# Layer 2's scan: delta*u of every fourth unit by an fp32 product on PE, y stores on ACT's queue

## The reference

```
def step(state, inp):
    d, b, c, uu = inp
    dA = jnp.exp(d[..., None] * A_neg[:, None, :, :])
    state = dA * state + (d * uu)[..., None] * b[:, :, None, :]
    y = jnp.einsum('kbcn,kbn->kbc', state, c)
    return (state, y)
```

## Time and profile before

| | |
|---|---|
| median of 3 runs | 17231.57 us (17228.62 to 17241.57) |
| profiled execution | 17236.15 us |
| its span, first to last instruction | 17234.5 us |
| scan of layer 2 | 8540 to 15594 us of the span |
| granted PE clock, mean over the span | 0.833 |
| PE busy over the span | 12704.4 us (74%) |
| DVE busy | 11266.0 us (65%) |
| ACT busy | 7765.1 us (45%) |
| POOL busy | 6782.0 us (39%) |

### The profile page before, as it was taken

One profiled execution on the slowest core, in us unless ns is written; L12 is line 12 of the kernel. 1 busy time (PEld: TensorE's weight loads), 2 busy tenths in 40 slices (PEclk: granted clock), 3 DMA queues, 4 the chain that ended last, 5 costly groups with the idle time before them and its releaser, 6 DMA issues. The chain is left out here.

```text
span 17234.5 us, 361490 instructions
## 1 busy us (share of the span) xinstructions
PE 12704.4 (74%) x127392; PEld 8742.7 (51%) x127392; DVE 11266.0 (65%) x10439; ACT 7765.1 (45%) x13769; POOL 6782.0 (39%) x3199
## 2 busy tenths in 40 slices
PE   7889999888999954454466666666666666667799
PEld 5666666666666632222244444444444444444477
DVE  5666666666666655555477777777777777775532
ACT  4444444444444434544455545554555545552200
POOL 1000000000000014423577777887778877772100
PEclk9999999999999977777677777777777777776799
DMA  5222222222222237766899999999999999998711
GB/s 124 65 57 58 59 59 53 66 56 66 59 59 59 53 106 186 179 153 159 209 233 233 234 230 233 235 235 234 236 232 235 237 228 232 233 230 222 197 39 40
DMA packets 2038805, 2633.89 MB, mean 153 GB/s; under 512 B 1083612, under 2 KB 1935324, under 8 KB 2013404
## 3 DMA queue, kind: packets, MB, share of 16 engines
q1 hardware_dynamic: 1991388, 2487.10, 59.5%
q0 software_dynamic: 12288, 86.71, 2.3%
q10 hardware_dynamic: 34944, 57.81, 1.2%
HBM read 2103.61 MB, written 556.32 MB: 154 GB/s over the span
## 5 line engine op out<-in xcount | busy, mean ns | idle before, releaser
L1731 DVE TENSOR_TENSOR_SCAN L2.h<-L2.ps,L2.db 128x912 f32<-128x912 f32 x2688 | 5515.0, 2056 | 1569.2 <-POOL L2.db L1587 1522.1
L1587 POOL TENSOR_TENSOR L2.db<-L2.du,L2.bt 128x896 f32<-128x896 f32 x2688 | 5580.1, 2096 | 1551.7 <-DMA L2.du<-du 1468.0
L1608 PE MATMUL L2.ps<-L2.dm,L2.wa 32*128 32x112 f32 x21504 | 2306.9, 346 | 2471.1 <-DVE L2.h L1731 2343.4
L1669 ACT ACTIVATE L2.ps<-L2.ps 128x896 f32<-128x896 f32 x2688 | 2424.5, 902 | 3503.4 <-PE L2.ps L1608 3501.6
L1608 PEld LDWEIGHTS L2.ps<-L2.dm,L2.wa 32*128 32x128 f32 x21504 | 1899.6, 246 | 3268.2 <-DVE L2.h L1731 2940.3
L1621 PE MATMUL L2.ps<-L2.h,L2.cd 128*8 128x96 f32 x50176 | 2575.6, 362 | 5.5 <-DVE L2.h L1731 5.5
L1621 PEld LDWEIGHTS L2.ps<-L2.h,L2.cd 128*8 128x8 f32 x50176 | 1439.4, 108 | 583.6 <-DVE L2.h L1731 5.6
L314 POOL TENSOR_TENSOR L1.x_res<-L1.x_res,L1.ob 96x3136 f32 (+1 forms) x16 | 95.4, 5977 | 2582.2 <-ACT L1.qv L457 2582.2
L314 POOL TENSOR_TENSOR L0.x_res<-L0.x_res,L0.ob 96x3136 f32 (+1 forms) x16 | 95.9, 6007 | 2367.8 <-ACT L0.qv L457 2367.8
L366 PE MATMUL L1.p_proj<-L1.xt,L1.w_hi 128*96 128x448 f32 x3024 | 826.4, 383 | 194.2 <-DVE L1.xt L560 167.5
L366 PE MATMUL L0.p_proj<-L0.xt,L0.w_hi 128*96 128x448 f32 x3024 | 826.3, 383 | 194.3 <-DVE L0.xt L560 167.6
(11 more groups left out here) (255 smaller groups left out, 19811.4 us busy)
## 6 DMA issues: line engine op xcount, KB each, us to landing
L2.du<-du SPq DMA_DIRECT2D x5376, 224.0 KB, 6.6
L2.dm<-d SPq DMA_DIRECT2D x896, 336.0 KB, 6.8
y<-L2.ysum SPq DMA_DIRECT2D x896, 84.0 KB
L0.left<-table SPq DMA_DIRECT2D x48, 1176.0 KB
L0.right<-table SPq DMA_DIRECT2D x48, 1176.0 KB
L1.left<-table SPq DMA_DIRECT2D x48, 1176.0 KB
L1.right<-table SPq DMA_DIRECT2D x48, 1176.0 KB
du<-L2p.work SPq DMA_DIRECT2D x64, 784.0 KB, 7.5
```

What stands on the lines that cost most here:

```text
L1587: pool.tensor_tensor(db[:, n % RB, :, 2:ROW], du[:, n % RD, :].rearrange("p (c t) -> p c t", t=SPAN), row, ALU.mult)\
L1608: mm = pe.matmul(decays[n % RA][:, lo:lo + SPAN], wa[rows, u * QUAD + e, :], dm[rows, u * QUAD + e, :], start=True, stop=True)
L1669: act.activation(a, a, ACT.Exp).then_inc(a_ready, 1)
L1731: dve.tensor_tensor_scan(h[:, half, u * UNIT:(u + 1) * UNIT, :].rearrange("p c t -> p (c t)"), decays[n % RA], db[:, n % RB, :, :].rearran ...
```

## The change

In the scan of layer 2:
- Units with n % 4 = 3 (six of a span's 24) get no `load_du`. SP loads the eight images' rows once (`load_few`, two runs of 1,792 B for each of 8 partitions) into `few`, which has two slots. It is issued at unit n = 4i for unit 4i + 3. PE multiplies them with `fan`, an 8 x 128 matrix of zeros and ones, in fp32 (`fan_out`): two products of 448 columns, at the ends of units 4i and 4i + 1, both into bank 7. ACT copies each into the unit's slot of `du` (`copy_du`) before the decay of units 4i + 1 and 4i + 2. POOL waits for these copies (`du_copied`) instead of a transfer.
- The sums have bank 6 alone; `sum_states` waits until ACT has taken the fill before.
- On ACT `take_sum` stands before the unit's decay and carry instead of behind them.
- `ysum` has one buffer. Its stores are issued from ACT's queue, behind u = 11 of the half in which the sums were made (and before `make_cd`), and ACT waits at u = 4 of the next half for the stores to have landed.

```
+        def by_pe(n):
+            return n % 4 == 3
...
-                    load_du(k, s, half, u)
-                    if u == 2 and earlier is not None:
-                        sp.wait_ge(sum_out, fills + (2 - FILLS))
-                        steady(sp)
-                        store_y(*earlier, half)
+                    n = half * UNITS + u
+                    if n % 4 == 0:
+                        load_few(k, s, n // 4)
+                    if not by_pe(n):
+                        load_du(k, s, half, u)
...
+            def fan_out(i, g, k, s):
+                copies = count(pe, k, s, 2 * FANS, 2 * i + g)
+                if g == 0:
+                    pe.wait_ge(few_in[i % 2], count(pe, k, s, 16 * FANS // 2, 16 * (i // 2 + 1)))
+                if not (isinstance(copies, int) and copies == 0):
+                    pe.wait_ge(du_copied, copies)
+                pe.matmul(ps[:, 7, 0:QUAD * SPAN], fan[:], few[:, i % 2, g * QUAD * SPAN:(g + 1) * QUAD * SPAN],
+                          start=True, stop=True).then_inc(fanned, 1)
...
-                bank = 6 + (half * FILLS + f) % 2
-                pe.wait_ge(sum_out, fills + (f + 1))
+                pe.wait_ge(sum_out, fills + (f + 2))
...
                         sum_states(1 - half, f, before)
+                    n = half * UNITS + u
+                    if n % 4 < 2:
+                        fan_out(n // 4, n % 4, k, s)
...
+            def copy_du(i, g, units, copies):
+                n = 4 * i + 3
+                act.wait_ge(fanned, copies + (2 * i + g + 1))
+                act.wait_ge(b_ready, units + (n + 1))
+                act.copy(du[:, n % RD, g * QUAD * SPAN:(g + 1) * QUAD * SPAN], ps[:, 7, 0:QUAD * SPAN]).then_inc(du_copied, 1)
...
                 for u in range(UNITS):
-                    decay(half * UNITS + u, spreads)
-                    carry(half, u, units, begun)
                     f = u - FIRST_FILL - 1
                     if 0 <= f < FILLS and not first:
                         if f == 0:
-                            act.wait_ge(y_stored[1 - half], count(act, k, s, 64, 64 * half))
+                            act.wait_ge(y_stored[half], count(act, k, s, 64, 64))
                         take_sum(k - 1 if begun and half == 0 else k, 1 - half, f, before)
+                    n = half * UNITS + u
+                    if 1 <= n % 4 <= 2:
+                        copy_du(n // 4, n % 4 - 1, units, copies)
+                    decay(n, spreads)
+                    carry(half, u, units, begun)
+                if not first:
+                    act.wait_ge(sum_out, before + (FILLS + 2))
+                    steady(act)
+                    if half:
+                        store_y(k, s, 0)
+                    elif begun:
+                        store_y(k - 1, NSPANS - 1, 1)
+                    else:
+                        store_y(k, act.snap(s - 1), 1)
                 if half == 0:
                     make_cd(k, s, before)
```

More of the change, by code:

```diff
@@ L1420, in scan_layer @@
         db = m.sb("db", [128, RB, UNIT, ROW])
-        ysum = m.sb("ysum", [128, 2, SPAN // 4, HALF])
+        ysum = m.sb("ysum", [128, SPAN // 4, HALF])
+        few = m.sb("few", [BATCH, 2, UNIT * SPAN])
+        fan = m.sb("fan", [BATCH, 128])
         zero = m.sb("zero", [128, UNIT])
@@ L1432, in scan_layer @@
         bt_in = [m.sem(f"bt_in{s}") for s in range(2)]
+        few_in = [m.sem(f"few_in{s}") for s in range(2)]
+        fanned = m.sem("fanned")
+        du_copied = m.sem("du_copied")
         image_in = m.sem("image_in")
@@ L1454, in count @@
             return eng.snap(s * scale + (k * NSPANS * scale + add))
+        def by_pe(n):
+            return n % 4 == 3
+        FANS = 2 * UNITS // 4
+        moved = [[n for n in range(2 * UNITS) if n % RD == q and not by_pe(n)] for q in range(RD)]
         def span_of(s):
@@ L1488, in load_cc, with load_few @@
                 sp.dma_start(cc[:], bc_dram[1, k].rearrange("b n t -> (b n) t")[:, span_of(s)]).then_inc(cc_in, 16)
+            def load_few(k, s, i):
+                before = count(sp, k, s, 2 * FANS, 2 * (i - 1))
+                n = 4 * i + 3
+                c = n // UNITS * HALF + n % UNITS * QUAD
+                rows = du_dram[k, :, 0, 0:NSPANS * CH * SPAN].rearrange("b (s g n) -> b s g n", s=NSPANS, n=SET * SPAN)
+                g0, at = c // SET, c % SET * SPAN
+                rows = rows[:, s, g0:g0 + 2, at:at + QUAD * SPAN] if isinstance(s, int) else \
+                    rows[:, bass.ds(s, 1), g0:g0 + 2, at:at + QUAD * SPAN].rearrange("b a g n -> b (a g) n")
+                if not (isinstance(before, int) and before <= 0):
+                    sp.wait_ge(fanned, before)
+                steady(sp)
+                sp.dma_start(few[:, i % 2, :].rearrange("b (g n) -> b g n", g=2), rows).then_inc(few_in[i % 2], 16)
             def load_du(k, s, half, u):
@@ L1499, in load_du, with half_span @@
                     sp.dma_start(du[:, slot, g * QUAD * SPAN:(g + 1) * QUAD * SPAN], src).then_inc(du_in[slot], 16)
[L1501 to L1510, removed]
+            def half_span(k, s, half, later, table):
                 units = count(sp, k, s, 2 * UNITS, half * UNITS)
-                fills = count(sp, k, s, 2 * FILLS, half * FILLS)
                 for u in range(UNITS):
@@ L1578, in span @@
                 units = count(pool, k, s, 2 * UNITS)
-                loads = count(pool, k, s, 32 * 2 * UNITS // RD)
+                loads = {q: count(pool, k, s, 32 * len(moved[q])) for q in range(RD) if moved[q]}
+                copies = count(pool, k, s, 2 * FANS)
                 for half in range(2):
@@ L1584, in span @@
                         n = half * UNITS + u
[L1585 removed]
+                        if by_pe(n):
+                            pool.wait_ge(du_copied, copies + 2 * (n // 4 + 1))
+                        else:
+                            pool.wait_ge(du_in[n % RD], loads[n % RD] + 32 * (moved[n % RD].index(n) + 1))
                         pool.wait_ge(scanned, units + (n + 1))
@@ L1655, in _, with store_y @@
             act.wait_ge(cleared, 1)
-            act.wait_ge(image_in, 16)
+            act.wait_ge(image_in, 32)
+            def store_y(k, s, half):
+                for q in range(4):
+                    at = s * SPAN + SPAN // 4 * q
+                    if k % 2:
+                        at = at * -1 + (TOK - SPAN // 4)
+                    rows = slice(at, at + SPAN // 4) if isinstance(s, int) else bass.ds(at, SPAN // 4)
+                    place = y_dram[k, :, rows, half * HALF:(half + 1) * HALF]
+                    act.dma_start(place, ysum[32 * q:32 * q + BATCH, :, :]).then_inc(y_stored[half], 16)
             def make_cd(k, s, fills):
```

27 lines of the change are left out of this document (14 added, 13 removed).

## The result

The changed kernel takes 16,749.85 us (median of four runs, 16,740.79 to 16,755.04), beside 17,234.71 us (17,228.62 to 17,241.57) for the kernel before on the same chip. The ratio is 0.9724, with a 95% interval of 0.9712 to 0.9736: 485 us less, where 17,250 us, no change, had been forecast. The profiled execution has a span of 16,739.1 us. Times "on the mean" or "as a median" over halves are taken over 107 halves of each kind (half 0, half 1) in the profiled execution of the kernel named.

The account below looks back on a forecast made before the run. Du loads over DMA bound layer 2's scan; afterwards a PE and ACT chain of 31.1 us per half, 31.3 with late loads, times 224 plus 5 and some 35 gives 7,051 against 7,054 us: 17,250 us, range 16,600 to 17,750.

Parts of the forecast that it names:

- What bounds the kernel now, and what DMA would do: Layer 2's scan: du loads set the pace; all bytes fall 17.5%, DMA share to 0.83 to 0.88, at most 1,230 us gained.
- The price of four y issues on ACT (4.5 us): End of each half on ACT: four stores hold its queue 4.5 us, the empty-queue value plus address work.
- rival C: Slower: ACT's stores alternate with SP's du packets, so issues lengthen; 17,450 to 18,050 us, chance 0.28.
- The 4.6 us that the prediction names as its point: Issue time for four stores on ACT from which the slower rival was said to decide.
- rival B: Faster: stores hold ACT only for their shortest issues, or the clock alone is high; 16,100 to 17,000 us, chance 0.25.
- Two decays with carries at 0.90 each, until 24.4; stores 4.5, until 28.9.: End of a half on ACT: last decays and carries, then stores, one after another, in us from its first scan.
- 0.59 + 1.57 + 0.80 = 2.96 us: PE unit at full clock: spread, sum and product in series, against DVE's 2.06 us.
- The rest of the sum: Remainder of the half's chain over PE and ACT, which gave 29.9 us, 32.3 with make_cd, mean 31.1.
- the allowances for late loads, the last fills, the changes of direction and the rounding: Added to layer 2's scan: 0.2 us per half, 5 us, some 35 us; then the total rounded up to 17,250 us.
- The rule on issuing engines: Stores on ACT: by the skill's "usually small" they would be near their shortest issues and the half 3 us shorter.

Follow-up runs that it names:

- act_stores: Kernel before the change, with only the y stores moved to ACT's queue behind u = 11 (two ysum buffers and two PSUM banks kept); 16,996.43 us, ratio 0.9864.
- spread_issue: Changed kernel with the four y stores still on ACT's queue but issued one each behind u = 10, 11, 0 and 1; 16,353.01 us, ratio 0.9491.
- late_issue: Changed kernel, but ACT waits before the four y stores until its own last carry (u = 11) is done; 17,169.82 us, ratio 0.9964.
- same_rows: Changed kernel with half 1's product operands on partitions 64 to 71, the rows of its spread, half 0's as before; 17,021.19 us, ratio 0.9877.
- same_late: Changed kernel with half 1's product operands on partitions 64 to 71 and stores issued only behind ACT's last carry; 17,362.37 us, ratio 1.0078.
- products_alone: Changed kernel with y stores back on SP's queue at u = 2 and two ysum buffers; products stay on PE with single banks; 16,508.97 us, ratio 0.9583.
- sp_spread: Kernel before the change, y stores still on SP's queue but one each at u = 2, 3, 4 and 5; 17,285.43 us, ratio 1.0038.

## Why the prediction was wrong, by its steps

**What bounds the kernel now, and what DMA would do.** Right. du was the pace, POOL's waits for it went from 1,194 us to 127 (under 400 had been said), and DVE's waits moved to ACT's carry. DMA's share came out at 0.91, above 0.83 to 0.88, since the half is shorter than forecast.

**The price of four y issues on ACT (4.5 us).** Right: 4.54 and 4.59 us. The reason given for it, an empty queue, is not shown, and the agreement is in part luck: in act_stores, with the same four stores in a row on ACT's queue, they take 3.1 us on the mean. The rival C did not occur. The 4.6 us that the prediction names as its point is a slip: at 224 us for each us above 4.5, C's interval from 17,450 begins at (17,450 - 17,250) / 224 + 4.5 = 5.4 us. The rival B did not occur either, though the time falls into its interval: the stores in a row were not at their shortest, and the clock did not help, since the spreads of u = 2 and 3 took 1.10 us in half 1 (12031.70 and 12033.38), the length at the low level. spread_issue shows that B's 0.28 us per store is about what a spaced store costs.

**"Two decays with carries at 0.90 each, until 24.4; stores 4.5, until 28.9."** This step failed. It puts ACT's issuing behind ACT's computing as if both were one. In half 0 the times before it are right: the decay of u = 10 began 22.25 us into the half (22.6 in the prediction), and the last carry ended at 24.2 (24.4). But the stores began at 22.9 and not at 24.4, with the decays and carries of u = 10 and 11 beside them. late_issue restores the serial order and costs 427 us, some 60 of them for its own wait. The chain behind the stores is a little longer than reckoned: half 0 from their end to the next scan takes 12031.27 - 12027.70 = 3.6 us with make_cd (3.4 in the prediction), half 1 1.55 (1.0).

**"0.59 + 1.57 + 0.80 = 2.96 us" for a PE unit with a product.** The mechanism, that PE sets DVE's pace from u = 3 to 9, was right, and the term is right in half 0 (2.90). In half 1 it was mis-sized: 2.51. A unit without a product takes 2.24 us (12044.04 to 12046.28; 2.16 in the prediction), so the product adds 0.66 us in half 0 and 0.27 in half 1, where the prediction had 0.80 for both. same_rows takes the overlap of half 1 away and costs 278 us. In half 1 the spread of u = 10 begins at 12050.38, 19.1 us into the half and not 21.9, its decay at 20.6, and the last carry ends at 22.5.

**The rest of the sum.** The two causes are worth 626 us together, and the kernel without them, same_late, stands 112 us above the forecast. The 500 us between forecast and result are thus made of two errors of opposite sign, of which the larger is explained by the two overlaps. In the trace of same_late the chain at the end of a half is longer than in the sum by 0.1 us up to the last carry, by 0.25 for its own wait in front of the stores, and by 0.2 (half 0) and 0.55 (half 1) behind them (medians), 0.7 us on the mean of the two halves. That is more than the 0.5 us per half of the run, so the allowances for late loads, the last fills, the changes of direction and the rounding were together about 0.2 us too large; they were not measured one by one.

**What the sum did not have.** The gain of a second queue for y. Its 241 us alone, and the 713 us of the products alone, do not add: together the two parts give 485 us, 228 less than the products alone. The waits suggest why. Both parts relieve the same wait, POOL's for du (per unit scanned 0.52 us before, 0.46 in act_stores, 0.25 in products_alone, 0.05 in the changed kernel), and once it is nearly gone the stores' time on ACT stands on the chain.

**The rule on issuing engines.** The Trainium skill (DMA: Bandwidth & Descriptors, section Issuing engines are not separate DMA queues) says that the sequencer's time for an issue is "usually small relative to the DMA itself", and that issuing from several engines saves this time alone. In a row it was not small for this kernel: 4.5 us for four stores of 84 KB each, on a half of 29 us; spaced, at 0.28 us for most, it was. The second part is in doubt here: in act_stores DMA moved 241 GB/s against 233, while saving SP's issue time alone, in sp_spread, left it at 232.

**The rows of the array.** The Trainium skill (TensorEngine Tiling (Array Packing), section Key Properties) states that tiles operate independently, and that different tiles can run their weight loads and matmuls in parallel. The trace agrees, with 2.51 us beside 2.90: here it held for an 8-row product and 32-row products that have nothing to do with one another. The prediction gave the product one price for both halves and did not ask which rows it takes.

## What to carry to other kernels

Before adding a small product on PE, see which rows the matmuls next to it use, and put its operands on others: here that was worth 241 us. When DMAs move to an engine that also computes, give its queue in the trace a timeline of its own, since it runs ahead of the compute, and space the issues out: four in a row cost 4.5 us, four spread over four units 1.4. And two edits that relieve the same wait need not be worth the sum of what each brings: here 713 and 241 us alone made 485 together.

## What was not expected of the hardware

- A matmul on rows 0 to 7 ran beside all eight matmuls on rows 64 to 127, and only partly beside matmuls on rows 0 to 63: 2.51 against 2.90 us for the unit, and so in the medians over all halves (2.52 and 2.90).
- ACT's sequencer issued stores 1.3 to 1.8 us before the end of ACT's own earlier instructions; holding it back cost 427 us, some 340 of them for the overlap itself.
- Issuing one store took 0.28 us on ACT's queue in most cases when the stores were spaced. Four in a row took 4.5 us on the mean (4.1 to 5.0) in the changed kernel, up to 8.3 in late_issue, but 3.1 on the mean in act_stores; why they differ is open.
- With 5% of the bytes moved to a second queue, and their stores to another place, DMA moved 241 GB/s instead of 233, and the shares of the two queues add up to 1.08.
